# One Trainium2 core, an audio tower block: where the input x and its parts enter

## The chip, the cores and the metric

The kernel runs on one core of a Trainium2 chip. The time is device microseconds of one execution. Five engines work side by side and meet at semaphores: TensorE (PE; its weight loads are PEld), VectorE (DVE), ScalarE (ACT), GpSimd (POOL) and SyncE (SP). SP only issues DMAs; ACT issues some as well. The DMAs of all queues are carried out by 16 DMA engines.

## The reference, cut to what matters

x has the shape (32, 4, 250): 32 sequences, 4 input dims, 250 positions. The first layer makes from it a state of 64 values for each position and refines it 8 times, from the left and from the right:

```python
a = jnp.einsum('bdl,od->blo', x, W1) + b1
for _ in range(8):
    up = relu(a + shift_r(up) @ W2.T + b2)
    down = relu(a + shift_l(down) @ W2.T + b2)
c = jnp.einsum('bdl,od->blo', x, W3) + b3
miu = relu(c + (shift_r(up) @ W4.T + b4) + (shift_l(down) @ W4.T + b4))
```

After it come a residual attention layer with 8 heads whose scores are exp(-gamma * squared distance), and a residual mixture of experts (16 experts, top 2) with a layer norm. Only the first layer reads x.

## The kernel before, in words

The work has three stages: A (the first layer, L964 to L1049), B (attention) and C (experts). The trace has A up to about 106 us. The change is all in the stretch before A's loop has got going.

The products with x are made in bfloat16 without losing float32 precision: x is split into PARTS = 3 bfloat16 parts whose sum is x, and the weights are too. Each x term is one matmul over XROWS = 3 * 3 * 4 = 36 rows (every part of x against every part of the weights, for 4 dims) and 3 further rows that hold a constant for the bias. So rows 0 to 35 and 64 to 99 of the tiles `xa` and `xw` hold x (the second half in reversed order of positions), and rows 36 to 38 and 100 to 102 a constant, ONES2. Rows 32 to 63 and 96 to 127 are filled with the constant first, and the x rows are then written over them by DMA.

How x gets there:

1. SP issues the load of x into `x_in` (L265). Behind it, on the same queue, it issues the seven A_LOADS (L267): `c_sb`, `aw1_sb`, `aw2_sb`, `cw1_sb`, `cw2_sb` (these four are 103 rows of 256 bytes), `w24_sb` and `gam_sb`.
2. DVE fills rows 96 to 127 of `xa` and `xw` (L657, L658), then waits for x and splits it into `x_part` in four steps (L661 to L667). POOL fills rows 32 to 63 (L330, L331), then makes 24 small fills at the edges of the state tiles (L335 to L338; PREP_GA counts them), then two long fills of `m2` (L341).
3. SP waits for the split and for POOL's two fills (PREP_GX), writes `x_part` to the DRAM buffer `xparts` (L271), waits until it has landed, and issues four reads of it for round 0 (`replicate`, L277): `xa` in two halves and `xw` in two halves. Each read writes 36 partitions. Its source has the shape [3 copies, 12 rows, n * 500 elements], where the 12 rows are (part, dim). Behind them SP issues the eleven B_LOADS (L287), and then the four reads of round 1.
4. ACT waits for x, issues the four W_LOADS (L490), waits for PREP_GA and then relieves PSUM. The instruction ACT_TABLE_LOAD stands ahead of its first activation (L498).
5. DVE waits for all A_LOADS and makes the bfloat16 parts of the first layer's weights (L670 to L676, PREP_A = 5). Then, in `weights()` (L680 to L692, PREP_W = 8), it waits for PE's weight products and takes them out of PSUM (L688, L691). Only then does it relieve PSUM in stage A (L700).
6. PE waits for the W_LOADS, makes the weight products (L966, L967), waits for PREP_A and PREP_GA, and begins stage A. `step_a` (L995) with k = 0 waits for the reads into `xa`, and for lane 3 for PREP_W; with k = 1 it waits for both evacuations of its lane (a_sa by ACT, a_sb by DVE) and for the reads into `xw`. There are 4 lanes and 2 rounds.

Of the kernel before, what the change touches and what calls it, by code (L numbers as in the profile page):

```python
# [8 lines left out]
ACT = mybir.ActivationFunctionType  # L9
AX = mybir.AxisListType  # L10
F32 = mybir.dt.float32
# [4 lines left out]
B, D_IN, L = 32, 4, 250  # L16
# [9 lines left out]
C = 2 * L  # L26
# [10 lines left out]
PARTS = 3  # L37
XROWS = PARTS * PARTS * D_IN
AROWS = XROWS + PARTS
HALF = 64  # L40
XK = HALF + AROWS
ONES2 = 1.0019378662109375
# [12 lines left out]
def constants():  # L55

    c = np.zeros((128, C_COLS), np.float32)
    c[:, C_IDENT:C_IDENT + 128] = np.eye(128)

    for half in (0, HALF):  # L60
        for part in range(1, PARTS):
            rows = slice(half + part * PARTS * D_IN, half + (part + 1) * PARTS * D_IN)
            for r in (rows, half + XROWS + part):
                c[r, C_W1] = -1.0
                c[r, C_W2] = -1.0 if part == 2 else 0.0
    c[64:, C_MS1] = -1.0
    c[Q_ROW + H:Q_ROW + 2 * H, C_MS2] = -1.0
    c[K_ROW + H:K_ROW + 2 * H, C_MS2] = -1.0
    for a in (1, 3):
        c[a * E:(a + 1) * E, C_MG] = -1.0  # L70
    for h in range(H):
        c[K_ROW + h, C_IND + h] = 1.0
        c[K_ROW + H + h, C_IND + h] = 1.0
    for e in range(E):
        c[e, C_SEL + e * R:C_SEL + (e + 1) * R] = 1.0
        c[E + e, C_SEL + e * R:C_SEL + (e + 1) * R] = 1.0
    return c


def build(nc, cst, xin, xparts, aw1, aw2, cw1, cw2, w24, wqT, wkT, wvT, woT, wq, wk, gam, lns,  # L80
          gw, gb, w1, b1, w2, b2, fg, fb, out):
    with ExitStack() as ctx:
        def sb(name, shape, dt=F32):
            return ctx.enter_context(nc.sbuf_tensor(name, shape, dt))

        def sem(name):
            return ctx.enter_context(nc.semaphore(name))

        def f32(ap):
            return ap.bitcast(F32)  # L90
# [27 lines left out]
        spare, spare2 = sb("spare", [T, 1]), sb("spare2", [T, 1])  # L118
# [55 lines left out]
        ld_w, ld_a, ld_b = sem("ld_w"), sem("ld_a"), sem("ld_b")  # L174
        s_prep = sem("s_prep")
        s_prepg = sem("s_prepg")
        s_wprod = sem("s_wprod")
        a_xin, a_split, a_scr = sem("a_xin"), sem("a_split"), sem("a_scr")
        a_xa = [sem(f"a_xa{i}") for i in range(ROUNDS)]
        a_xw = [sem(f"a_xw{i}") for i in range(ROUNDS)]  # L180
        a_mm, a_sa, a_sb, a_c, a_miu, a_t, a_h = (
# [16 lines left out]
        def full(t):  # L198
            return t[tuple(slice(None) for _ in t.shape)]

        def wait(eng, s, value):

            if not (isinstance(value, int) and value <= 0):
                eng.wait_ge(s, value)
# [3 lines left out]
        A_LOADS = [(c_sb, cst), (aw1_sb, aw1), (aw2_sb, aw2), (cw1_sb, cw1), (cw2_sb, cw2),  # L208
                   (w24_sb, w24), (gam_sb, gam)]
# [6 lines left out]
        def steps(eng, step, body):  # L216

            first, last = body
            for p in range(first):
                step(p, p % 2, p >= 2, p >= 1, True, True)  # L220
            with eng.Fori(0, (last - first) // 2) as i:
                for k in range(2):
                    step(i * 2 + (first + k), (first + k) % 2, True, True, True, True)
            for p in range(last, PAIRS + 2):
                step(p, p % 2, p - 2 < PAIRS, p - 1 < PAIRS, p < PAIRS, p + 1 < PAIRS)
# [37 lines left out]
        @block.sync  # L263
        def _(sp):
            sp.dma_start(x_in[:, :, :], xin[:, :, :]).then_inc(a_xin, 16)  # L265
            for dst, src in A_LOADS:
                sp.dma_start(full(dst), full(src)).then_inc(ld_a, 16)  # L267

            sp.wait_ge(a_split, SPLIT)
            sp.wait_ge(s_prepg, PREP_GX)  # L270
            sp.dma_start(xparts.rearrange("r p (q l) -> q r p l", q=128), x_part[:, :, :, :]).then_inc(a_scr, 16)  # L271
            sp.wait_ge(a_scr, 16)

            def replicate(dst, half, rev, p0, n, s, d0):
                cols = slice(p0 * C, (p0 + n) * C)
                src = xparts[rev, :, :].rearrange("p (d c) -> (p d) c", d=D_IN)[:, cols]
                sp.dma_start(dst[half:half + XROWS, d0 * C:(d0 + n) * C],  # L277
                             src.unsqueeze(0).to_broadcast([PARTS, PARTS * D_IN, n * C])).then_inc(s, 16)

            for i in range(ROUNDS):  # L280
                for half, rev in ((0, 0), (HALF, 1)):
                    replicate(xa, half, rev, 2 * LANES * i, 2 * LANES, a_xa[i], 2 * LANES * i)
                for half, rev in ((0, 1), (HALF, 0)):
                    replicate(xw, half, rev, 2 * LANES * i + LANES, LANES, a_xw[i], LANES * i)
                if i == 0:
                    for dst, src in B_LOADS:
                        sp.dma_start(full(dst), full(src)).then_inc(ld_b, 16)  # L287


            def duplicate(p, j, u):  # L290
                sp.wait_ge(b_ev, 16 * p + 9 + 2 * u)
                for a in range(2):
                    sp.dma_start(f32(m1[j][64 - 64 * a:128 - 64 * a, 2 * u + a, :]),
                                 f32(m1[j][64 * a:64 * a + 64, 2 * u + a, :])).then_inc(b_dup[u], 16)


            def step_b(p, j, old2, old, new, ln):
                if new:
                    duplicate(p, j, 0)
                    duplicate(p, j, 1)  # L300
                    sp.wait_ge(b_s2, p + 1)
                    wait(sp, b_sc, 16 * (p - 1))
                    for k in range(2):
                        sp.dma_start(f32(m2[j][ONE_ROW + k:ONE_ROW + k + 1, :, :]),
                                     f32(s2[j][Q_ROW + k * H:Q_ROW + (k + 1) * H, :])).then_inc(b_row, 16)
                    duplicate(p, j, 2)
                    duplicate(p, j, 3)

            steps(sp, step_b, BODY_B)


            with sp.Fori(0, PAIRS) as i:
                sp.wait_ge(c_pout, i + 1)
                sp.dma_start(out[ds(i * 2, 2), :, :].rearrange("b (k t) d -> t (b k) d", k=2), res[:, :, :])\
                    .then_inc(c_out, 16)
            sp.wait_ge(c_out, 16 * PAIRS)
# [3 lines left out]
        def _(gp):  # L320
            count = [0]

            def done(ins):

                count[0] += 1
                ins.then_inc(s_prepg, 1)
                gp.wait_ge(s_prepg, count[0])


            done(gp.memset(xa[32:64, :].bitcast(F32), ONES2))  # L330
            done(gp.memset(xw[32:64, :].bitcast(F32), ONES2))  # L331
            assert count[0] == PREP_GX
            for j in range(LANES):
                for t in (st_a[j], st_b[j]):
# [150 lines left out]

        @block.scalar
        def _(act):
            act.wait_ge(a_xin, 16)
            for dst, src in W_LOADS:
                act.dma_start(full(dst), full(src)).then_inc(ld_w, 16)  # L490
# [156 lines left out]
        def _(dve):  # L647
# [6 lines left out]
                dve.wait_ge(s_prep, count[0])  # L654


            dve.memset(xa[96:128, :].bitcast(F32), ONES2)  # L657
            dve.memset(xw[96:128, :].bitcast(F32), ONES2)  # L658

            dve.wait_ge(a_xin, 16)  # L660
            dve.tensor_copy(x_part[:, :, 0, :], x_in[:, :, :]).then_inc(a_split, 1)  # L661
# [589 lines left out]
SPLIT = 4  # L1251
PREP_A = 5
PREP_W = 8
PREP_GX = 2
PREP_GA = PREP_GX + 6 * LANES
PREP_G = PREP_GA + 26
GATE_D = 9
# [72 lines left out]
```

## Time and profile before

| | |
|---|---|
| median of 3 runs | 883.58 us (882.91 to 884.26) |
| profiled execution, time | 883.49 us |
| its span, first to last instruction | 881.3 us |
| PE busy | 799.4 us (91%) |
| DVE busy | 770.7 us (87%) |
| ACT busy | 593.7 us (67%) |
| POOL busy | 458.0 us (52%) |
| mean granted TensorE clock | 0.987 |

The span is cut into 40 slices of 22 us on the page. PE's digit is 1 in the first, 6 in the second and 8 or 9 from the third to the 39th. A slice's digit is the busy share in tenths.

### The profile page before, as it was taken

The page shows a single profiled execution, that of the slowest core. Times are in us where ns is not written, and L with a number is a line of the kernel's source. Part 1 is how long each engine was busy: PE and PEld are TensorE (multiplying, and loading weights), DVE is VectorE, ACT ScalarE, POOL GpSimd, SP SyncE. Part 2 cuts the span into 40 slices and gives each one's busy share as a digit, 9 for nine tenths or more (in the row PEclk, how much of TensorE's full clock was granted, in tenths as well). Part 3 has the DMA queues.
Part 4 walks back from the last instruction along what each step waited for, and adds up shares of the span by engine and source line. Part 5 has one row for each costly group of instructions (what it writes and reads, how often), then busy time and mean ns, then how long its engine had stood idle before and what let it go on. Part 6 is the DMA issues. An engine that isn't in the chain of part 4 may idle for free.

```text
span 881.3 us, 17428 instructions
## 1 busy us (share of the span) xinstructions
PE 799.4 (91%) x4384; PEld 456.0 (52%) x4384; DVE 770.7 (87%) x1970; ACT 593.7 (67%) x1089; POOL 458.0 (52%) x600
## 2 busy tenths in 40 slices
PE   1699879999999999999999998899999999999994
PEld 1244356666666666666666655344444444444441
DVE  5376769999999999999999998899999999999984
ACT  0365678778788788788788775566666666666652
POOL 7270255435445445445544421267776667777655
PEclk9999979999999999999999999999999999999998
DMA  4400022111222111222111220000000000000000
GB/s 115 134 16 2 1 49 47 27 37 38 49 48 48 24 36 36 48 48 48 25 38 34 49 49 1 0 5 9 6 6 6 6 6 7 6 6 6 9 10 12
DMA packets 22742, 25.16 MB, mean 29 GB/s; under 512 B 12753, under 2 KB 21649, under 8 KB 22577
## 3 DMA queue, kind: packets, MB, share of 16 engines
q1 hardware_dynamic: 22384, 23.93, 11.5%
q10 hardware_dynamic: 320, 0.79, 0.4%
q8 instruction: 18, 0.29, 0.1%
q14 instruction: 20, 0.16, 0.1%
HBM read 5.37 MB, written 2.43 MB: 9 GB/s over the span
## 4 chain that ended last, share of the span: by engine, by line
PE 54%; DVE 16%; issue 15%; POOL 7%; ACT 4%; DMA 2%; SPq 1%; POOLq 1%; DVEq 0%; ACTq 0%
PE bank L1178 9%; PE bank L1196 9%; PE bank L1063 8%; PE bank L1111 6%; PE bank L991 6%; PE bank L1087 4%; DVE gated L258 3%; PE bank L1089 3%; DVE prob L773 3%; DVE lg L866 2%; DMA xw<-xparts 2%; DVE m L789 2%; PE bank L981 1%; DVE lg L870 1%; POOL xn L409 1%
## 5 line engine op out<-in xcount | busy, mean ns | idle before, releaser
L773 DVE TENSOR_SCALAR prob<-prob,cap_hi,cap_lo 125x250 f32<-125x250 f32 x512 | 231.4, 500 | 16.9 <-ACT prob L542 14.2
L607 ACT ACTIVATE relu<-bank,b_sb 128x500 f32<-128x500 f32 x256 | 161.1, 675 | 101.5 <-PE bank L1196 86.4
L420 POOL TENSOR_TENSOR sq<-sq 125x256 f32<-125x256 f32 x128 | 97.5, 767 | 166.1 <-ACT sq L556 109.9
L542 ACT ACTIVATE prob<-bank 125x500 f32<-125x500 f32 x256 | 148.3, 590 | 41.0 <-PE bank L1089 37.7
L258 DVE TENSOR_TENSOR gated<-relu,wb 128x500 f32<-128x500 f32 x224 | 159.9, 728 | 7.7 <-ACT relu L607 5.5
L1178 PE MATMUL bank<-gated,w_sb 128*64 128x500 f32 x512 | 136.0, 610 | 12.6 <-DVE gated L258 12.6
L1063 PE MATMUL bank<-prob,u 125*64 125x250 f32 x1024 | 125.0, 382 | 1.9 <-DVE prob L773 1.8
L1087 PE MATMUL bank<-m,s 128*125 128x500 f32 x256 | 110.9, 433 | 4.1 <-issue 1.9
L1196 PE MATMUL bank<-s,w_hi 128*128 128x500 f32 x256 | 110.6, 432 | 0.0
L1089 PE MATMUL bank<-m,s 112*125 112x500 f32 x256 | 101.3, 396 | 0.0
L1196 PE MATMUL bank<-s,w_lo 128*128 128x500 f32 x256 | 99.5, 388 | 0.0
L1063 PEld LDWEIGHTS bank<-prob,u 125*64 125x64 f32 x1024 | 66.2, 136 | 55.3 <-issue 16.8
L789 DVE TENSOR_TENSOR m<-bank,m 64x500 fp32r<-64x500 f32 x128 | 86.3, 674 | 3.7 <-ACT m L551 1.4
L556 ACT ACTIVATE sq<-bank 125x512 f32<-125x512 f32 x128 | 76.2, 600 | 19.5 <-POOL sq L420 16.8
L1111 PE MATMUL bank<-wqku_hi,s 128*125 128x512 f32 x192 | 77.6, 404 | 6.4 <-DVE m L789 3.9
L1196 PEld LDWEIGHTS bank<-s,w_hi 128*128 128x128 f32 x256 | 48.4, 189 | 59.3 <-ACT relu L607 54.4
L1111 PE MATMUL bank<-wqku_lo,s 128*125 128x512 f32 x192 | 76.8, 400 | 0.0
L551 ACT ACTIVATE m<-bank 64x500 fp32r<-64x500 f32 x128 | 74.0, 578 | 0.8
L1087 PEld LDWEIGHTS bank<-m,s 128*125 128x125 f32 x256 | 48.0, 187 | 36.9 <-issue 29.3
L700 DVE TENSOR_SCALAR st_b<-bank 128x500 f32<-128x500 f32 x56 | 37.3, 678 | 29.2 <-PE bank L991 22.1
L991 PE MATMUL bank<-st_a,w_sb 64*64 64x500 f32 x224 | 58.7, 594 | 0.0
L991 PE MATMUL bank<-st_b,w_sb 64*64 64x500 f32 x224 | 57.8, 595 | 0.0
(176 smaller groups left out, 1476.8 us busy)
## 6 DMA issues: line engine op xcount, KB each, us to landing
m<-m SPq DMA_DIRECT2D x128, 125.0 KB, 2.3
out<-res SPq DMA_DIRECT2D x16, 125.0 KB
xa<-xparts SPq DMA_DIRECT2D x4, 281.2 KB
w1raw<-in_w SPq DMA_DIRECT2D x1, 1024.0 KB
xw<-xparts SPq DMA_DIRECT2D x4, 140.6 KB
w_sb<-in_w SPq DMA_DIRECT2D x1, 512.0 KB
m<-s SPq DMA_DIRECT2D x32, 15.6 KB
xparts<-x_part SPq DMA_DIRECT2D x1, 375.0 KB, 4.3
```

The lines of the kernel that those rows point to most:

```text
L258: eng.tensor_tensor(gated[g % 8][:, :], relu_sb[g % 4][:, :], wb[j][:, :], ALU.mult).then_inc(s_done, 1)
L542: act.activation(prob[n % PROBS][:, :, :], bank[5 + n % 3][0:T, 0:C].rearrange("p (h l) -> p h l", h=2), ACT.Exp).then_inc(b_exp, 1)
L607: act.activation(relu_sb[g % 4][:, :], bank[4 + g % 4][:, 0:C], ACT.Relu, bias=b1_sb[:, g:g + 1]).then_inc(c_relu, 1)
L773: last = dve.tensor_scalar(part, part, cap_hi[0:T, h:h + 1], cap_lo[0:T, h:h + 1], ALU.min, ALU.max)
L789: last = dve.tensor_tensor(m2[j][0:64, h, :], bank[2 + k % 3][rows, 0:C], f32(m1[j][rows, h, :]), ALU.subtract)
L991: last = pe.matmul(dst[cols, 0:C].rearrange("p (b l) -> p b l", b=2), w24_sb[rows, 0, :], src[rows, :, 0:L], start=False, stop=True)
L1063: last = pe.matmul(bank[1][64 * c:64 * c + 64, 0:L], u_sb[jj][:, 2 * b + c, h * D:(h + 1) * D], prob[(2 * v + c) % PROBS][:, hh, :], start ...
L1087: pe.matmul(ps, s1[o][:, cols], m1[o][:, 2 * hp:2 * hp + 2, b * L:(b + 1) * L], start=True, stop=False)
L1089: pe.matmul(ps, s2[o][:, cols], m2[o][:, 2 * hp:2 * hp + 2, b * L:(b + 1) * L], start=False, stop=True).then_inc(b_sc, 1)
L1111: last = pe.matmul(dst[0:T, :], s1[j][:, c * T:(c + 1) * T], w[:, q, :], start=first, stop=not first)
L1178: last = pe.matmul(y[64 * k:64 * k + 64, 0:C], w2_sb[:, g, :], gated[g % 8][:, :], start=False, stop=v == 7, skip_group_check=True)
L1196: last = pe.matmul(bank[4 + g % 4][:, 0:C], w[:, g, :], s1[o][:, :], start=first, stop=not first)
```

## The change

A_LOADS are issued by ACT as its first instructions; SP's queue then holds x_in, the write of `xparts` and the reads. ACT does one activation of a single column ahead of its wait for x; DVE clears that column for it. POOL makes all four fills of constant rows (PREP_GX = 4) and DVE none. SP waits for POOL's fills behind the landing of `xparts`, no longer ahead of its write. The source of each read has the shape [12 rows, 3 copies, n * 500]: the three copies of a row now lie in neighbouring partitions, and the rows of the weights (`stacked`) and of the constants are laid out to match.

```diff
-            rows = slice(half + part * PARTS * D_IN, half + (part + 1) * PARTS * D_IN)
+            rows = slice(half + part, half + XROWS, PARTS)
@@ block.sync
             sp.dma_start(x_in[:, :, :], xin[:, :, :]).then_inc(a_xin, 16)
-            for dst, src in A_LOADS:
-                sp.dma_start(full(dst), full(src)).then_inc(ld_a, 16)
-
             sp.wait_ge(a_split, SPLIT)
-            sp.wait_ge(s_prepg, PREP_GX)
             sp.dma_start(xparts.rearrange("r p (q l) -> q r p l", q=128), x_part[:, :, :, :]).then_inc(a_scr, 16)
             sp.wait_ge(a_scr, 16)
+            sp.wait_ge(s_prepg, PREP_GX)
@@ replicate
-                             src.unsqueeze(0).to_broadcast([PARTS, PARTS * D_IN, n * C])).then_inc(s, 16)
+                             src.unsqueeze(1).to_broadcast([PARTS * D_IN, PARTS, n * C])).then_inc(s, 16)
@@ block.gpsimd
-            done(gp.memset(xa[32:64, :].bitcast(F32), ONES2))
-            done(gp.memset(xw[32:64, :].bitcast(F32), ONES2))
+            for rows in (slice(32, 64), slice(96, 128)):
+                done(gp.memset(xa[rows, :].bitcast(F32), ONES2))
+                done(gp.memset(xw[rows, :].bitcast(F32), ONES2))
@@ block.scalar
+            for dst, src in A_LOADS:
+                act.dma_start(full(dst), full(src)).then_inc(ld_a, 16)
+            act.wait_ge(a_table, 1)
+            act.activation(spare2[:, :], spare[:, :], ACT.Relu)
             act.wait_ge(a_xin, 16)
@@ block.vector
-            dve.memset(xa[96:128, :].bitcast(F32), ONES2)
-            dve.memset(xw[96:128, :].bitcast(F32), ONES2)
+            dve.memset(spare[:, :], 0.0).then_inc(a_table, 1)
@@ constants and stacked()
-PREP_GX = 2
+PREP_GX = 4
-                o[r * HALF:r * HALF + XROWS] = np.tile(w.T, (PARTS * PARTS, 1))
+                o[r * HALF:r * HALF + XROWS] = np.tile(np.repeat(w.T, PARTS, axis=0), (PARTS, 1))
```

## Rows read from the trace of the kernel before

**Rows 1.** Chain of waits, start and length in us, and what
```profile
10.74 4.34 DMA xparts<-x_part
...
15.10 0.87 SPq L277
...
17.47 14.42 DMA xw<-xparts
...
32.02 0.59 PE bank L981
...
32.66 1.67 PE bank L991 x8
...
38.72 0.84 PE bank L991 x8
```

**Rows 2.** Timeline of SP's queue: start us, us, engine, line, operation
```profile
0.76 0.41 SPq L265 DMA_DIRECT2D x_in<-in_xin  x1
...
2.82 3.32 SPq L267 DMA_DIRECT2D cw_sb<-in_cw  x2
...
6.19 3.96 SPq L267 DMA_DIRECT2D w_sb<-in_w  x1
...
10.19 0.43 SPq L267 DMA_DIRECT2D gam_sb<-in_gam  x1
```

**Rows 3.** Timeline of ACT and its queue
```profile
3.48 0.56 ACTq L490 DMA_DIRECT2D wqv_sb<-in_wqT  x1
...
5.42 0.62 ACTq L490 DMA_DIRECT2D wko_sb<-in_woT  x1
...
26.92 1.28 ACT L498 ACT_TABLE_LOAD   x1 [26.92 <-PE bank L984]
```

**Rows 4.** Timeline of DVE and POOL, idle time before and its releaser in brackets
```profile
0.75 3.42 POOL L330 MEMSET xa<- 32x4000 f32 x1 [0.29 <-POOLq L1319]
...
5.41 1.73 DVE L658 MEMSET xw<- 32x2000 f32 x1 [0.36 <-issue]
...
6.04 0.11 POOL L335 MEMSET st_a<- 128x2 f32 x1
...
7.15 0.42 DVE L661 CAST x_part<-x_in 128x500 bf16<-128x500 f32 x1
...
8.77 0.68 DVE L667 TENSOR_TENSOR x_part<-x_res,x_part 128x500 bf16<-128x500 f32 x1
...
10.07 0.10 POOL L338 MEMSET sh<- 64x2 f32 x1
...
10.23 6.91 POOL L341 MEMSET m<- 32x4000 f32 x2
...
14.99 2.23 DVE L672 CAST awr<-awt 103x128 bf16<-103x128 f32 x1
...
17.64 0.23 DVE L675 CAST awr<-awt 103x128 bf16<-103x128 f32 x1
...
19.45 0.68 DVE L691 COPY wraw<-bank 128x512 f32<-128x512 f32 x1
...
26.97 2.44 DVE L700 TENSOR_SCALAR st_b<-bank 128x500 f32<-128x500 f32 x4 [6.84 <-PE bank L984]
```

**Rows 5.** Stretches: busy time of each engine, PEclk, DMA share, GB/s
```profile
9.00:9.50 0.50, 0.00 (x0) 0.00 (x0) 0.45 (x1) 0.00 (x0) 0.33 (x4) 1.00 0.07 19
...
22.00:22.50 0.50, 0.00 (x0) 0.00 (x0) 0.00 (x0) 0.00 (x0) 0.00 (x0) 1.00 0.15 64
...
128.00:132.00 4.00, 4.00 (x11) 3.10 (x10) 3.17 (x11) 3.11 (x7) 0.23 (x1) 0.52 0.00 0
```

**Rows 6.** DMA issues on the page: KB each
```profile
xa<-xparts SPq DMA_DIRECT2D x4, 281.2 KB
```

**Rows 7.** Groups by line, 11 to 26 us: busy, mean ns, idle before
```profile
L966 PE MATMUL bank<-wko_sb,wqv_sb 64*128 64x64 f32 x16 | 3.7, 420 | 11.8 <-DMA wko_sb<-in_woT 11.8
```

**Rows 8.** Waits, 34 to 110 us: total us, times, longest
```profile
POOL inv L390 <- DVE aggr L738: 27.9, 1, 27.9
```

More of the change, by code:

```diff
@@ L177, in build @@
         s_wprod = sem("s_wprod")
-        a_xin, a_split, a_scr = sem("a_xin"), sem("a_split"), sem("a_scr")
+        a_xin, a_split, a_scr, a_table = sem("a_xin"), sem("a_split"), sem("a_scr"), sem("a_table")
         a_xa = [sem(f"a_xa{i}") for i in range(ROUNDS)]
```

## The prediction

> **What bounds the kernel now.** I began with the page's busy digits: PE is at 1 and 6 in the first two slices and at 8 or more afterwards, so the part of the kernel that the change touches is a stretch in which PE waits. Then the chain of waits over the first 80 us [rows 1]. It says what PE waited for: SP issues its loads, `xparts` is written (10.74, 4.34 us), the four reads are issued from 15.10, and the last of them, into `xw`, is waited for 14.42 us. From 32.02 on the chain lies on PE without a gap until stage A ends near 106 us. So whatever moves the first matmul of step k = 1 (now 32.02) moves everything behind it by the same amount, until another engine or load is late. That instant is what I compute.
>
> Three more views say what each part of the wait is made of. The timeline of SP's queue [rows 2] shows that issuing alone keeps SP busy from 0.76 to 10.62: one load, `w24`, holds it for 3.96 us. The stretch of 9.00 to 9.50 [rows 5] lies in it: DMA share 0.07, which is about one of 16 engines (0.0625), at 19 GB/s. The queue is held by transfers that one engine does. The timeline of DVE and POOL [rows 4] shows that x was split late, 7.15 to 9.45, because DVE filled rows until 7.14. And the stretch at 22.00 [rows 5], in which only the reads are under way, has share 0.15, at most three engines of 16, and 64 GB/s.
>
> **The reads.** They have 3 outer copies before and three engines' worth of traffic; 12 outer rows should give 12 engines. The four of round 0 move 843.6 KB, or 864,000 bytes (two of 281.2 KB into `xa` [rows 6], two of half that into `xw`). They take from the first issue at 15.10 to 32.02, which is 16.9 us. At 64 GB/s this volume needs 13.5 us, so 3.4 us are issue and latency. With four times the engines the transfer takes 13.5 / 4 = 3.4 us, and the last issue now matters: the four issues take from 15.10 to 17.43. I expect the last read about 5.7 us after the first issue; bounds 3.4 (transfer free) and 16.9 (nothing gained).
>
> The Trainium skill, DMA: Bandwidth & Descriptors, section "Why a DMA increments its semaphore by 16 and not by 1", says that a DMA from SP or ACT runs on the largest number of engines up to 16 that divides the slowest dimension of both sides: 3 of (3, 36) before, 12 of (12, 36) after. By that rule the trace's 0.15 agrees (3/16 is 0.19), and 103 rows, a prime, go on one engine, which agrees with the 0.07. Its section "Issuing engines are not separate DMA queues" speaks against the other edit: issuing from a second engine saves only sequencer time, "usually small relative to the DMA itself". By that rule the queue edit moves nothing: the reads would start at 15.1 as now, the last land 5.7 later at 20.8, and W_LOADS be no later than now, so k = 1 at 20.9, 11.1 us earlier, and 870.9 with the clock's share below. The trace disagrees about "small": SP's issue of the seven loads takes 9.4 us. I give this case no more than 2 in 100.
>
> **x, its split and the fills.** x lands by 3.48, when ACT, which waits for it, issues its first load [rows 3]. DVE no longer fills 5.1 us of rows first. But POOL now fills all four: 3.42 + 1.76 + 3.42 + 1.76 us and gaps, from 0.75 to about 11.3 (DVE's fill of `xw` took 1.73, POOL's 0.03 more) [rows 4]. Do DVE's casts and POOL's fills run side by side? L672's cast took 2.23 us, from 14.99 to 17.22, and POOL's long fill ended at 17.14; the equal cast of L675 took 0.23 [rows 4]. So a cast between two SBUF tiles waits until POOL's fill is over. Worked out: first cast from 3.5 ends at 4.6 (behind the fill that ends at 4.17), subtraction to 5.3, second cast behind the fill of `xw` (now to 6.4) ends at 6.8, last subtraction at 7.5. POOL's fills lose 0.4 us twice and end at 12.0. The write of `xparts` is issued at 7.5 and takes 4.34 as now: landed at 11.9. Then SP waits for the fills, 12.0. The reads start at 12.0 in place of 15.10 (bounds 10.2, if nothing collides and the fills alone decide at 11.3 or less; 13.5, if every cast waits for a long fill). The last one has landed at 12.0 + 5.7 = 17.7.
>
> **What is late next: the weight products.** So far k = 1 could start at 17.8, a gain of 14. It can't, for what I expect of ACT's queue. W_LOADS are issued now from 3.48 to 6.04 [rows 3], the products wait for them until 11.84 and take 3.7 us [rows 7]. After the change they stand behind seven A_LOADS and the activation with its table load.
> - ACT's seven issues: at most SP's 9.4 us (0.8 to 10.2), since their one-engine transfers then ran against W_LOADS on that engine, which now come later; at least seven at 0.6 us, the length of ACT's own [rows 3], to 5.0. `cw1` and `cw2` held SP for 3.32 us and `w24` for 3.96 [rows 2]; I take 8.3, nearer to the upper end.
> - Table load 1.28 us [rows 3] and a short activation, 0.2: W_LOADS start at 9.8.
> - From their first issue to the products: 8.4 us now (3.48 to 11.84), of which a part is the shared engine. At least 2.6 us of issuing and 2.7 as x_in took (0.76 to 3.48), 5.3. They now meet the `xparts` write and the first reads. I take 6.4: products start at 16.2.
> - Products 3.7: 19.9. DVE's L691 takes 0.68 [rows 4] and L688, of the same 128x512 from PSUM, as much: 21.3. DVE's first evacuation, a quarter of 2.44 [rows 4], with its hand-over: 0.7. So k = 1 starts at 22.0, in place of 32.02: **10.0 us gained**.
>
> Beside this: A_LOADS landed by about 10 to 11, so L670 to L676 (2 us without a blocked cast) end before 14, unless a cast meets a fill. POOL's 24 small fills take 4.1 us (6.04 to 10.17) and end at 16.1: PREP_GA comes before the products end. Its long fills of `m2` then run from 16.1 to 23; DVE has by then only PSUM reads, which the trace doesn't show blocked. The reads into `xa` (17) come before 19.9. The table load is 0 on the path before (hidden in the wait for `xw`) and 1.3 to 1.5 in the chain above. B_LOADS start earlier by about 3 us and finish earlier; POOL's preparation has 27.9 us of idle time behind it [rows 8], so nothing of it comes on the path.
>
> **The clock.** The two first steps of k = 1 run at half rate: eight L991 matmuls take 1.67 us against 0.84 later [rows 1], 2.1 us lost with their x terms. That is the 1.2 GHz level, behind a wait of PE for `xw`. After the change PE is busy from 16.2 to 21 with products and x terms, with short gaps, so the clock may already be full at 22.0, or rise a step or two later. Bounds 0 and 2.1, I take 1.5. Further on there are half-rate stretches at the seam of A and B, like 128 to 132 with 0.52 [rows 5]. Where they fall may shift by a few us; a shift of a stretch by 3.4 us is worth 1.7 us, either sign. Mean 0.
>
> **Sum.** 10.0 + 1.5 = 11.5 us off the profiled execution's 883.49 (span 881.3 and 2.2 around it): 872.0. The median of the runs, 883.58, is 0.1 above that execution; I leave it.
>
> **Rivals.**
> 1. ACT's queue is as slow as SP's was: issues to 10.2, table to 11.7, products 8.4 later at 20.1, k = 1 at 25.9. Gain 6.1, no clock gain: 877.4. For it: the one-engine transfers are the same. Against: their competitor on that engine is gone while they run.
> 2. The reads stay as narrow: last one at 12.0 + 16.9 = 28.9, gain 3.1, 880.4. For it: the bytes and destinations are unchanged, and 36 destination rows may be the limit. Against: the share 0.15 for three copies and 0.07 for 103 rows.
> 3. **Slower.** W_LOADS, queued behind A_LOADS, come so late that the products end behind 32. This decides from a product start of 26.2, that is a first W issue at 17.8 with 8.4 us behind it: the seven issues would need 15.5 us in place of 9.4. If sharing the first engine with x_in, the `xparts` write and the reads doubled them (18.8), products would start at 29.5, k = 1 at 35.3: 3.3 us slower, 886.8. For it: SP was held for 3.96 us by a single load. Against: 19 GB/s on one engine is a light load, and x needs little of it.
> 4. A_LOADS decide, not W_LOADS: a cast of DVE's preparation is caught behind one or both 3.4 us fills of `m2`. PREP_W comes at 24.5, gain 6.8: 876.7 before any clock gain. For it: L672. Against: it needs A_LOADS later than 14.
>
> **Chances.** Forecast 0.74, the queue edit worth nothing 0.02, rival 1 0.08, rival 2 0.05, rival 3 0.03, rival 4 0.05, and 0.03 for a gain returned at the seam so that less than 0.2% is left. 0.2% (1.8 us) is what a measurement of this kernel can tell from no change. So faster 0.94, same 0.03, slower 0.03. The fast end: issues to 7.0, table to 8.5, products 5.3 later, k = 1 at 19.6, gain 12.4, clock 2.1, seam 1.5: 867.5. The slow end takes in rivals 1 and 4: 877.5.
>
> **What would show it.** In the trace after: the stretch with the reads at a DMA share near 12/16; the `xparts` issue near 7.5 and first read near 12.0; ACT's first W issue near 9.8; products starting near 16.2; the first L991 near 22.0 and waiting for DVE's evacuation, not for a DMA; L991's first eight at 0.84 or a little over. I am wrong if k = 1 waits for `xw`, or if PE's start moves by 10 us and the end doesn't.

## The result: 873.53 us, 10 us faster

The changed kernel takes 873.53 us (median of 4 runs, 873.05 to 874.62) against 883.58 (four runs, 882.91 to 884.26): ratio 0.9888, 95% interval 0.9871 to 0.9905. The forecast was 872.0 with a range of 867.5 to 877.5. The profiled execution took 874.62 with a span of 872.5; against the 881.3 of before that is 8.8 us less. The ratios of the table further down leave out one run of the kernel before, of 1293.1 us at a granted clock of 0.567. The page's first part and PE's digits:

```profile
span 872.5 us, 17430 instructions
PE 799.6 (92%) x4384; PEld 455.4 (52%) x4384; DVE 768.1 (88%) x1969; ACT 593.4 (68%) x1090; POOL 462.6 (53%) x602
...
PE   1999889999999999999999998899999999999994
```

PE's busy time is the same within 0.2 us; its second digit went from 6 to 9. The chain of waits (start, length, what; lines of the kernel are one further on than before) has where stage A starts:

```profile
22.98 0.59 PE bank L982
...
24.86 0.38 PE bank L982
...
25.28 1.67 PE bank L992 x6
...
28.70 0.84 PE bank L992 x7
```

The first four pieces of L982, from 22.98, are step k = 0 of the four lanes; step k = 1 follows without a gap, its first matmul at 24.62 by the timeline, in place of 32.02 [rows 1]. It no longer waits for `xw`; what it waits for is `xa`, since k = 0 comes only at 22.98. The last group of transpositions of stage A starts at 98.31 in place of 106.21. So 7.9 of the 8.8 us are there when stage A ends; the rest comes later, in pieces of 0.4 us and less. The timeline of the stretch, each with its engine, answers to [rows 2 to 4]:

```profile
0.76 0.42 SPq L265 DMA_DIRECT2D x_in<-in_xin  x1
...
4.23 1.76 POOL L329 MEMSET xw<- 32x2000 f32 x1
4.41 1.85 DVE L662 CAST x_part<-x_in 128x500 bf16<-128x500 f32 x1 [3.53 <-DMA x_in<-in_xin]
6.05 3.59 POOL L328 MEMSET xa<- 32x4000 f32 x1
...
7.01 2.90 DVE L666 CAST x_part<-x_res 128x500 bf16<-128x500 f32 x1
...
8.30 0.45 ACTq L487 DMA_DIRECT2D gam_sb<-in_gam  x1
8.79 1.28 ACT L489 ACT_TABLE_LOAD   x1 [8.79 <-issue]
8.87 0.53 ACTq L492 DMA_DIRECT2D wqv_sb<-in_wqT  x1
...
10.66 0.40 SPq L267 DMA_DIRECT2D xparts<-x_part  x1
...
16.08 0.47 PE L967 MATMUL bank<-wko_sb,wqv_sb 64*128 64x64 f32 x1 [16.08 <-DMA wko_sb<-in_woT]
16.64 1.76 SPq L274 DMA_DIRECT2D xa<-xparts  x2
...
22.98 0.59 PE L982 MATMUL bank<-xa,acw 39*64 39x500 bf16 x1 [3.23 <-POOL qkw L340]
```

The products start at 16.08 and end at 19.8; PE then stands idle 3.2 us, until `xa` is there. The trace names POOL's fill of `qkw` as releaser, which no instruction of PE waits for; it is the semaphore event nearest in time. The reads were issued at 16.64, and k = 0 needs those into `xa`. So in this trace x decides, and not the weight products, as the forecast had it. Both casts are long, 1.85 and 2.90 us against 0.42 [rows 4]: each starts inside one of POOL's fills and ends 0.27 us after the fill's end (5.99 and 6.26, 9.64 and 9.91).

The reads themselves are wide now. Stretches, columns as in [rows 5]:

```profile
7.50:8.00 0.50, 0.00 (x0) 0.00 (x0) 0.50 (x1) 0.00 (x0) 0.50 (x1) 1.00 0.08 18
...
19.00:19.50 0.50, 0.50 (x8) 0.50 (x6) 0.00 (x0) 0.00 (x0) 0.50 (x1) 1.00 0.74 240
```

In the second line, 0.74 of 16 engines is 12, at 240 GB/s where it was 64; the first, with only the 103-row loads under way, is about one engine (1/16 is 0.06) at 18 GB/s.

### The profile page after: what moved, and what is told of

It is laid out like the page before. It is cut to its first block, busy times and chain, and to the rows that moved or that the text cites. A ratio compares the mean times of both kernels' runs of the same rounds, so it can differ in the third digit from the quotient of the medians.

```text
span 872.5 us, 17430 instructions
## 1 busy us (share of the span) xinstructions
PE 799.6 (92%) x4384; PEld 455.4 (52%) x4384; DVE 768.1 (88%) x1969; ACT 593.4 (68%) x1090; POOL 462.6 (53%) x602
## 4 chain that ended last, share of the span: by engine, by line
PE 53%; DVE 17%; issue 16%; POOL 9%; ACT 4%; POOLq 1%; DVEq 0%; ACTq 0%
PE bank L1179 8%; PE bank L1197 8%; PE bank L1064 8%; PE bank L1112 6%; PE bank L992 6%; PE bank L1088 4%; DVE gated L258 4%; PE bank L1090 3%; DVE prob L774 3%; DVE lg L867 2%; PE bank L982 2%; DVE m L790 2%; DVE lg L871 1%; POOL xn L407 1%; PE bank L1187 1%
## 5 line engine op out<-in xcount | busy, mean ns | idle before, releaser
L774 DVE TENSOR_SCALAR prob<-prob,cap_hi,cap_lo 125x250 f32<-125x250 f32 x512 | 231.9, 501 | 16.2 <-ACT prob L544 13.5
L1179 PE MATMUL bank<-gated,w_sb 128*64 128x500 f32 x512 | 136.0, 610 | 12.2 <-DVE gated L258 12.2
L558 ACT ACTIVATE sq<-bank 125x512 f32<-125x512 f32 x128 | 76.3, 600 | 20.0 <-POOL sq L418 16.2
L500 ACT ACTIVATE st_a<-bank 128x500 f32<-128x500 f32 x56 | 32.2, 589 | 36.6 <-PE bank L992 23.2
```

Source lines behind the costliest of these rows:

```text
L774: last = dve.tensor_scalar(part, part, cap_hi[0:T, h:h + 1], cap_lo[0:T, h:h + 1], ALU.min, ALU.max)
L1179: last = pe.matmul(y[64 * k:64 * k + 64, 0:C], w2_sb[:, g, :], gated[g % 8][:, :], start=False, stop=v == 7, skip_group_check=True)
```

## The experiments

Each was timed in rounds with the kernel before; unless said otherwise each is an edit of the changed kernel. "x terms" is the start of PE's first x matmul, "end of A" the start of the last transpositions of the stage, both from the profiled execution. The kernel before had medians of 883.52 to 883.66 in these rounds. The changed kernel's two sets of runs (873.05 to 874.62, and 870.58 to 872.74) don't overlap: the same program differs by 2.2 us between rounds, so that a difference of 2 us between kernels of different rounds shows nothing.

| kernel | median us | ratio, 95% interval | products | x terms | end of A |
|---|---|---|---|---|---|
| before | 883.58 | | 11.84 | 26.19 | 106.21 |
| changed | 873.53 | 0.9888 (0.9871, 0.9905) | 16.08 | 22.98 | 98.31 |
| changed, again | 871.32 | 0.9859 (0.9844, 0.9874) | 15.35 | 19.20 | 95.78 |
| before + wide reads | 876.13 | 0.9921 (0.9904, 0.9939) | 12.31 | 21.66 | 98.39 |
| the same, again | 876.01 | 0.9916 (0.9902, 0.9929) | 12.25 | 23.03 | 100.32 |
| narrow reads | 879.50 | 0.9962 (0.9945, 0.9979) | 16.13 | 27.35 | 105.31 |
| tensor_tensor split | 873.09 | 0.9891 (0.9873, 0.9909) | 15.40 | 19.67 | 95.23 |
| DVE fills | 873.85 | 0.9896 (0.9878, 0.9914) | 15.56 | 21.81 | 97.73 |
| no early table load | 872.56 | 0.9890 (0.9859, 0.9920) | 16.00 | 20.00 | 97.87 |
| W_LOADS first | 876.02 | 0.9912 (0.9894, 0.9930) | 7.07 | 22.53 | 100.45 |
| full-height fills | 872.60 | 0.9872 (0.9850, 0.9893) | 15.63 | 19.96 | 96.01 |
| W first, full fills, split | 871.74 | 0.9867 (0.9845, 0.9888) | 7.49 | 18.74 | 94.86 |
| padded loads | 871.77 | 0.9866 (0.9842, 0.9890) | 10.42 | 18.95 | 94.95 |
| padded, full fills, split | 870.78 | 0.9852 (0.9837, 0.9867) | 10.66 | 18.82 | 93.62 |

**The width alone, twice.** The kernel before with

```diff
-                             src.unsqueeze(0).to_broadcast([PARTS, PARTS * D_IN, n * C])).then_inc(s, 16)
+                             src.unsqueeze(1).to_broadcast([PARTS * D_IN, PARTS, n * C])).then_inc(s, 16)
```

and the layouts that go with it.

> The kernel before with only the 12 outer rows in the reads (and the matching rows of weights and constants); queues and fills as before. Theory X (the x chain sets the start of stage A, and the width of the reads is nearly all of the gain): reads issued at 15.1 as before, xa landed 6.3 later at 21.4, step k=1 at about 23.1 against 24.65 in the changed kernel, so it is 1 to 2 us faster than the changed kernel, about 872. Theory Q (the queue and fill edits carry a real share): slower than the changed kernel, 876 or more.

Stage A ended as in the changed kernel, yet the times were 2.6 us apart. So both were run again, in the same rounds:

> The kernel before with wide reads alone, once more, in the same rounds as the changed kernel. Its stage A ended at 98.4 as the changed kernel's did (98.3), but its four times had a median of 876.1 against 873.5. Seam theory (the difference lies behind stage A, in where the half-rate stretches of the clock fall, which goes with the run): the two medians come within 1 us. Rival (queue and fill edits are worth 2 us and more): the gap of 2 to 3 us stays.

The gap was 4.7 us (876.01 against 871.32). Theory X and the seam theory fall: the queue and fill edits carry a real share. Of the 12.2 us of this comparison the width, taken first, has 7.5. SP's queue shows what else varies in this kernel, the issue of the 103-row loads. From the second trace:

```profile
1.68 1.77 SPq L267 DMA_DIRECT2D aw_sb<-in_aw  x2
3.50 4.48 SPq L267 DMA_DIRECT2D cw_sb<-in_cw  x2
...
12.04 0.43 SPq L267 DMA_DIRECT2D gam_sb<-in_gam  x1
...
16.41 1.71 SPq L277 DMA_DIRECT2D xa<-xparts  x2
```

The last of them, `gam`, goes out 1.9 us later than in [rows 2], the write behind it too (12.59 against 10.74), and the reads 1.3 us later (16.41 against 15.10). x was split at 9.45 in both, so the queue held its write for 3.1 us here and for 1.3 us there. Off that queue, x is free of it.

**The other edits alone.** The changed kernel with the narrow reads:

> The changed kernel with the reads back at 3 outer copies. Theory X: reads issued at 16.6 as in the changed kernel, the last landed 16.9 later at 33.5, so stage A starts later than before (32.0): about 885, 1 to 2 us slower than the kernel before. Theory Q: the queue and fill edits bring something without wide reads too: 880 or less.

Measured 879.50: theory Q, and about 4 us faster than before by the medians (3.4 by the ratio) without any wide read. The reads were issued at 16.28, 1.2 us later than before, and PE waited for both kinds:

```profile
PE bank L982 <- DMA xa<-xparts: 7.5, 1, 7.5
PE bank L982 <- DMA xw<-xparts: 2.4, 1, 2.4
```

The x terms come at 27.35, and k = 1 when `xw` is there, with its first state matmul at 32.03 (before 32.41). I had added before's 16.9 us; to the first matmul of k = 1 near 31.7 they took 15.4. Its ten times lie in two heaps, 877.4 to 878.7 (five) and 880.3 to 882.7 (five). The profiled one (881.7) is of the upper, with x split at 10.6 as in the first changed trace.

**The casts.** Both casts of the split as two-input operations with the same result:

```diff
-            dve.tensor_copy(x_part[:, :, 0, :], x_in[:, :, :]).then_inc(a_split, 1)
+            dve.tensor_tensor(x_part[:, :, 0, :], x_in[:, :, :], x_in[:, :, :], ALU.max).then_inc(a_split, 1)
```

> The changed kernel with the two casts of the split written as tensor_tensor max of a tile with itself (same values, 0.68 us each in place of 0.42). Lock theory (a cast between two SBUF tiles waits for GpSimd's fill, a two-input operation doesn't): split done at about 7.0 in place of 10.6, xparts written and landed near 11.5, reads start at 11.6, xa landed by 17.5; then the weight products, done at 19.8, with PREP_W at 21.2, bind: k=1 at 21.9, 2.7 us earlier than 24.65: about 870.8. Rival (the two operations are only slower beside fills, or the fills slow any DVE operation): split done at 10 or later, no gain.

The lock theory's step came out: the timeline has no long one, with the same fills beside it.

```profile
4.05 0.68 DVE L662 TENSOR_TENSOR x_part<-x_in 128x500 bf16<-128x500 f32 x1 [3.16 <-DMA x_in<-in_xin]
...
5.47 0.68 DVE L666 TENSOR_TENSOR x_part<-x_res 128x500 bf16<-128x500 f32 x1
...
6.90 0.40 SPq L267 DMA_DIRECT2D xparts<-x_part  x1
...
11.38 1.76 SPq L274 DMA_DIRECT2D xa<-xparts  x2
```

The write goes out 3.8 us earlier than in the first changed trace, and stage A ends 3.1 us earlier, at 95.23. Not all of that is the edit's: x was there at 4.05 in place of 4.41, and against a trace of the changed kernel in which it was there at 4.02 (below) the write is 0.3 and the end of A 0.5 us earlier. In that one a cast inside the same fill of `xw` took 1.23 us, the operation here 0.68. Two more things kept the gain small. POOL's last fill ran from 9.54 to 11.30, and the reads, which need it, went out at 11.38. And `xa` was there at 19.67, not at 17.5 as expected. The median, 873.09, is only 0.4 below the changed kernel's (expected 870.8); the step is shown by the trace, a gain in time is not.

**Fills back on DVE.**

```diff
+            dve.memset(xa[96:128, :].bitcast(F32), ONES2)
+            dve.memset(xw[96:128, :].bitcast(F32), ONES2)
```

> The changed kernel with rows 96 to 127 filled by VectorE again (before the split), PREP_GX back at 2. Lock theory: DVE's fills run beside GpSimd's from 0.9 to 6.0, the split runs 6.0 to 8.4 with only small fills beside it, in place of 4.4 to 10.6: reads start some 2 us earlier, k=1 at 22 to 22.7, about 871.5. Rival (moving the fills to GpSimd is worth its 5 us of DVE time, as the change assumes): slower than the changed kernel by 1 us or more.

Time the same as changed (873.85). The split ran unhindered, though only from 7.27, as DVE started its fills later than expected: 9.60 for the write, 21.81 for the x terms. The write is 1.1 us earlier than in the first changed trace and 2.4 later than in the second. Which of the two places is better depends on the next point. In this trace k = 1 did wait for `xw`, for 0.3 us until 24.02, so it has the only landing of the last wide read that can be seen: 9.1 us behind the first issue at 14.93. Against the kernel before with wide reads, timed in the same rounds, it is 2.3 us faster (873.22 to 874.70 against 875.06 to 876.92), and both fill rows on DVE; what differs is the queue of the A_LOADS, the early table load and the later wait for POOL. So these are worth something without the moved fills. That the moved fills are worth anything is not shown, and no run has the queue edit alone.

**The changed kernel again.**

> The changed kernel once more, to see how its start varies. Two-path theory (in the trace without the early table load x landed 0.5 us earlier and both casts waited for less: split done at 7.1, against 10.6; which fill a cast meets is decided by 0.5 us of x's landing): in this trace the first cast starts between 3.9 and 4.4, and if it starts before 4.2 the split ends near 7.2 and stage A near 95 to 96. Rival (the early activation or its DVE fill moves x): same as the first trace, cast at 4.4, split 10.6, stage A ends at 98.3. Time 873.5 either way within 1.

Here is the same program with x landed 0.4 us earlier:

```profile
4.02 0.43 DVE L662 CAST x_part<-x_in 128x500 bf16<-128x500 f32 x1 [3.14 <-DMA x_in<-in_xin]
4.23 1.92 POOL L329 MEMSET xw<- 32x2000 f32 x1
...
5.20 1.23 DVE L666 CAST x_part<-x_res 128x500 bf16<-128x500 f32 x1
...
7.17 0.40 SPq L267 DMA_DIRECT2D xparts<-x_part  x1
...
12.00 1.77 SPq L274 DMA_DIRECT2D xa<-xparts  x2
...
19.20 0.59 PE L982 MATMUL bank<-xa,acw 39*64 39x500 bf16 x1 [0.17 <-DMA xa<-xparts]
```

The first cast gets in before the fill of `xw` (which POOL now finishes late, 1.92), the second waits only for that fill and not for the next of 3.4 us. The split ends at 7.14 and not at 10.63. Here the reads needed both the write, landed just before 12.00, and POOL's last fill, over at 11.62. The two-path theory holds: of the six traces with these casts and POOL's fills beside them, the four whose first cast starts at 3.91 to 4.15 have the split done by 7.3, the two at 4.41 and 4.49 at 10.63. The expected time was 873.5 within 1; 871.32 is 2.2 below. That is the size of the step at the end of stage A (95.78 against 98.31), but which path the runs without a trace took is not known; that the two heaps of the narrow kernel are the same two paths fits too, and is not shown either. Why x lands later than before (3.48) is open. With W_LOADS issued beside its load, in place of A_LOADS, the first step of the split starts at 3.60 and 3.67 (two traces below), with A_LOADS beside it at 3.91 or later.

**Table load.**

```diff
-            act.wait_ge(a_table, 1)
-            act.activation(spare2[:, :], spare[:, :], ACT.Relu)
```

> The changed kernel without ScalarE's early activation and its wait (the table load then stands ahead of the first evacuation again). In the changed trace the table load (8.79 to 10.07) runs beside the issues of W_LOADS (first at 8.87), so removing it should not bring W_LOADS forward: products start at 16.1 as before. Theory T (the early load saves its 1.28 us on the first evacuation): ScalarE's first evacuation starts at 25.0 in place of 23.7, first L992-type matmul of k=1 at 26.0 in place of 25.0, stage A ends 1 us later at about 99.3, some 874.5. Rival (prediction's step: the table load delays W_LOADS by 1.3 to 1.5 us): products start at 14.8.

Its x took the short path, so it compares with the second changed trace. W_LOADS go out at 8.61 without the table load and at 8.87 or 8.82 with it, in which both stand side by side; the products don't start earlier (16.00). The load now takes 1.28 us ahead of the first evacuation:

```profile
20.73 1.28 ACT L498 ACT_TABLE_LOAD   x1 [20.73 <-PE bank L983]
22.02 2.03 ACT L498 ACTIVATE st_a<-bank 128x500 f32<-128x500 f32 x4
```

The first evacuation starts at 22.02 against 19.94, stage A ends at 97.87 against 95.78. Of these 2.1 us 0.8 were there at the x terms already and 1.4 at k = 1 (22.66 against 21.26), so the table load explains about 0.6; the last 0.7 came behind k = 1, where the slow first groups lasted longer (see the clock, below). The times (872.56 against 871.32 in other rounds) don't settle it.

**W_LOADS first.** The split as above, and ScalarE's two loops of DMAs in the other order, with W_LOADS no longer behind the wait for x:

> The split by tensor_tensor as in the run before, and ScalarE issues W_LOADS ahead of A_LOADS. Theory S (W_LOADS, when they run beside the xparts write or the reads, slow these: 5.9 us for the write in the changed kernel against 4.3 before, 8.3 us for the xa reads in the tensor_tensor run against 6.3): with W_LOADS gone by about 6 the write takes 4.3 to 4.4 and the xa reads 6.3: reads issued at about 11.8, first x term near 18.2, first k=1 state matmul near 20.2, stage A ends near 93.6 (98.3 in the changed kernel): about 869.5. Rival (the reads are slow by themselves, whatever runs beside them): xa lands at 19.7 or later, stage A ends at 95 or later.

A miss, and by neither theory. Products at 7.07, but the A_LOADS stand behind, and POOL's `m2` fills catch both casts of the preparation:

```profile
16.74 0.23 DVE L670 TENSOR_TENSOR awt<-aw_sb 103x64 f32<-103x64 f32 x1 [10.32 <-DMA gam_sb<-in_gam]
17.14 1.47 DVE L672 CAST awr<-awt 103x128 bf16<-103x128 f32 x1
...
19.03 3.06 DVE L675 CAST awr<-awt 103x128 bf16<-103x128 f32 x1
```

PREP_A comes at 22.5, and the x terms with it: 876.02, the slowest of the variants with wide reads on their own queue. This is the prediction's rival 4, made to happen. Whether W_LOADS slow the write and the reads stays open: from its issue to the first read the write took 4.4 to 6.0 us in the nine traces with the new queues in which it decided, 5.1 of them beside A_LOADS (W first with full fills), and 3.8 to 4.4 in the three of the old queue. Here, as in the run with the split alone, the reads went out at 11.38 only because POOL's last fill ended at 11.29.

**Fills of full height.**

```diff
-            for rows in (slice(32, 64), slice(96, 128)):
-                done(gp.memset(xa[rows, :].bitcast(F32), ONES2))
-                done(gp.memset(xw[rows, :].bitcast(F32), ONES2))
+            done(gp.memset(xa[:, :].bitcast(F32), ONES2))
+            done(gp.memset(xw[:, :].bitcast(F32), ONES2))
```

> The changed kernel with one fill of all 128 rows per tile in place of two of 32 rows (two fills in place of four; the x rows are written over by the reads). If a fill's time goes by columns alone: GpSimd's two fills end near 6.4 in place of 11.6. Lock theory: the first cast still waits for the xw fill (to about 6.2), the second meets only small fills: split done at 8.0 to 8.3 in place of 10.6, xparts issued at 8.1, reads at about 13, xa landed near 20.5, stage A ends near 96: about 871.5. Rival (the fill time goes by rows too): fills 4 times as long, worse than the changed kernel.

```profile
0.75 3.43 POOL L327 MEMSET xa<- 128x4000 f32 x1 [0.29 <-POOLq L1319]
4.24 2.03 POOL L328 MEMSET xw<- 128x2000 f32 x1
```

128 rows take what 32 rows take, so two of the four fills were for nothing. x took the short path (reads at 11.70), stage A ended at 96.01 and the median was 872.60, where 871.5 was expected; against the second changed trace (95.78) and its 871.32 no gain is shown. All three edits together:

> tensor_tensor split, W_LOADS first and full-height fills together. Fills end near 6; the write of xparts (near 7.2) and its landing (near 11.6) decide the reads, so stage A should start as with W_LOADS first alone: first x term near 18, stage A ends near 93.5, about 869.5. Rival: the long fills of m2 now run from about 10 to 17 and catch VectorE's two casts of the weight preparation (A_LOADS land near 12): PREP_A only near 17.5 to 18, stage A then starts at 18 to 18.5 because of PREP_A and not because of xa.

Stage A ends at 94.86, the x terms come at 18.74, 0.25 us behind PREP_A (18.49, by A_LOADS that landed at 16.8): 871.74, where 869.5 was expected. The fills of `m2` were over at 16.7 and caught no cast; the rival was right in PREP_A deciding, and not in why.

**Padded loads.** The four loads of 103 rows with 128, the tiles with them; the computation still reads 103:

```diff
-        o = np.zeros((XK, D), np.float32)
+        o = np.zeros((128, D), np.float32)
```

> The changed kernel with the four weight loads of 103 rows padded to 128 rows (25 rows of zeros more; the computation uses 103). One-engine theory (103 rows run on one DMA engine and hold the issuing queue): ScalarE's seven issues end near 4.3 in place of 8.75, W_LOADS are issued from 4.3, products start near 10 in place of 16.1, A_LOADS have landed by about 6. The write of xparts and the reads then no longer meet W_LOADS if the split ends at 10.6 (write 4.4 us, reads at 15.1, first x term near 21.4); with the split done at 7.2 they meet their tail. Stage A ends near 96 to 97: about 872. Rival (the seven issues are slow for another reason, the ScalarE queue itself): issues still end near 8.7, nothing moves.

```profile
2.18 0.94 ACTq L487 DMA_DIRECT2D cw_sb<-in_cw  x2
3.15 0.46 ACTq L487 DMA_DIRECT2D w_sb<-in_w  x1
3.63 0.45 ACTq L487 DMA_DIRECT2D gam_sb<-in_gam  x1
...
10.42 0.47 PE L967 MATMUL bank<-wko_sb,wqv_sb 64*128 64x64 f32 x1 [10.42 <-DMA wko_sb<-in_woT]
```

`cw` issues in 0.94 us in place of 4.64, `w24` in 0.46 in place of 1.40, and the products start 5.7 us earlier than in the first changed trace, 4.9 earlier than in the second. The one-engine theory holds. The time, 871.77, is that of the changed kernel in the same rounds (871.32): in its second trace x came 0.2 us behind the products, so with these gone x decides at once, 18.95 against 19.20, and k = 1 moves from 21.26 to 20.60. With the split and the full fills:

> Padding, tensor_tensor split and full-height fills together. x chain: split done at 6.9, write meets W_LOADS (data 5.5 to 9.5) and lands near 12, reads take 6.3 to 7: first x term near 18.5; products done near 14; A_LOADS near 6, so VectorE's casts come before the m2 fills. Nothing but the x chain is left: first k=1 state matmul near 20.3, stage A ends near 93.5 against 98.3: about 869. Rival (what stage A gains is given back at the seam to stage B): stage A ends near 93.5 but the time stays above 871.5.

The best start, with the end of A at 93.62, and the lowest median, 870.78; but 0.5 us under the changed kernel, with 870.6 to 872.7 and 869.6 to 872.0, is no difference shown; the expected 869 was missed, and the rival's 871.5 was not reached either. Only 0.8 of its lead at the end of A was there at k = 1 (20.50 against 21.26). The other 1.4 us is in how soon the state matmuls ran at full rate, here from the second group on:

```profile
21.12 1.61 PE bank L991 x8
...
22.95 0.84 PE bank L991 x8
```

Of the 2.2 us that its trace has over the second changed trace at the end of A, the spans (869.9, 870.6) keep 0.7. The rest goes behind stage A: 0.8 more at the seam to B, 1.1 from C's first matmul on, while B gives 0.4 back. Why there, no run tells.

## Why the prediction was right

**The reads** (forecast: four times as wide, last one 5.7 us after the first issue). Right in kind: 0.74 of the engines. In size they are slower: `xa` alone took 6.3 us in the first trace and up to 7.2 in the second, in which they meet W_LOADS; k = 1 waited for `xw` in neither, but all four took 9.1 us in the one trace that shows it (DVE fills). The term was too small because it added the issues of before, 2.3 us, and a quarter of the transfer, 3.4, and nothing for the time from an issue to the data; in before's 3.4 us of issue and latency it had been contained. The Trainium skill's rule on the slowest dimension (DMA: Bandwidth & Descriptors, "Why a DMA increments its semaphore by 16 and not by 1") gave 12 and 1 engines; the traces have 0.74 and 0.08 of 16, and padding 103 to 128 took the issue from 4.64 to 0.94 us.

**The split and the fills** (forecast: a cast waits for a fill; write at 7.5, reads at 12.0). The second trace has 7.17 and 12.00, the last by the write (4.83 us, forecast 4.34) and not by the fills, which ended at 11.62 and not at 12.0. In the first, x was there for the cast at 4.41, behind the start of the next fill at 4.23, and the same rule gives another schedule: 10.66 for the write. I had put x at 3.48; it came at 4.02 and 4.41. And I had let one order of events stand for the kernel, though a cast gets in only at the gap of 0.06 us between POOL's first two fills (4.17 to 4.23), and has to be there by then. My bound of 13.5 for the reads was passed, by 3.1 us, also because the write took 5.98 in place of 4.34.

**The products** (forecast 16.2, DVE's first evacuation behind PREP_W, k = 1 at 22.0). Measured 16.08 and 15.35. In the second trace k = 1 is at 21.26, and the chain of waits has what the forecast named, DVE's evacuation:

```profile
20.48 0.69 DVE st_b L701
...
21.26 0.59 PE bank L982
...
21.89 1.67 PE bank L992 x6
...
23.97 1.67 PE bank L992 x6
...
27.23 0.84 PE bank L992 x7
```

That 16.2 met 16.08 is luck, since its parts were off and cancelled: the table load, which I had put at 1.5 us ahead of W_LOADS, costs them nothing, since ACT's queue issues beside it; and ACT's seven issues took until 8.75 and W_LOADS 7.2 and 6.5 us from their first issue, not 8.3 and 6.4.

**The clock** (forecast: 1.5 us back). Not borne out. The first state matmuls still take 1.67 us for a group, twice the later 0.84, in both traces. Their x terms follow each other at 0.42 us for 500 columns, which is 1.2 GHz; but the granted clock of the view reads 1.00 in every stretch of the first 40 us, before as after, so the level is inferred from the durations, here and in the prediction. Stage A's end moved by 7.9 where k = 1 moved by 7.4, and by 10.4 where it moved by 10.8: 0.5 and -0.3. PE had been busy with products until 19.8 and then idle for 3.2 us in the first; in the second it had been busy since 15.35, the gap was 0.2 us, and the rate had still not risen at k = 1. The term was not a fixed one: over the fourteen traces the first group at full rate starts 2.5 us (padded, full fills, split) to 6.7 us (no early table load) behind k = 1, and 4.6 before, with no order by the edits that the traces show. From k = 1 to the end of stage A they take 73.1 (padded, full fills, split) to 75.2 us (no early table load), 74.2 before. So the 1.5 us had the right size for the best case, but not for the changed kernel, and about 2 us of any difference at the end of A can be this alone.

**The sum.** 10.0 + 1.5 forecast; 7.4 + 0.5 + 0.9 = 8.8 in the first trace; 10.8 - 0.3 + 0.3 (behind A) = 10.7 in the second, whose span is 870.6. So the time came out in the range by two routes. In the second trace the path was the forecast one, with k = 1 at 21.26 for 22.0 and the clock's share at nothing. In the first, which is of the runs that were forecast, x decided and k = 1 came 2.6 us late (24.62 for 22.0): there the wait that I had named was wrong, and when the products ended did not matter.

**The rivals:** the queue never was as slow as feared (issues end at 8.75, forecast 8.3), the reads did not stay narrow, nothing came near 32. Rival 4 happened only where A_LOADS were made late.

## What to carry to other kernels

Look at the outermost size of every DMA's two sides: 3 copies held the four reads for 15.4 to 16.9 us here, where 12 rows took 9.1, and 103 rows held a queue for 4.6 us, where 128 took 0.9. Before work is moved onto GpSimd, list the casts of VectorE that run beside it; here a saving of 5 us of fills could turn into 3.9 us of waiting, and the choice hung on half a microsecond of a load. When a step is made earlier, look for the second thing its successor waits for: with the casts freed, the reads waited for POOL's last fill. Two traces of one kernel are worth having where such a race is in it.

## What the runs showed of the hardware

- A fill of 128 x 4000 f32 on GpSimd takes 3.43 us, one of 32 x 4000 takes 3.42.
- A two-input operation of VectorE with a bfloat16 result (128 x 500, 0.68 us) isn't held by a GpSimd fill; a cast of the same tile is (0.42 alone, up to 2.90).
- The same with small tiles: casts of 103 x 128, 0.23 us alone, took 3.06 beside the fills of `m2`.
- ScalarE's queue issues DMAs while its table load runs (8.87 within 8.79 to 10.07).
- The reads at 12 engines moved 240 GB/s where 3 moved 64, yet from the first issue to the x terms `xa` took 11.1 us before (15.10 to 26.19) and 6.3 and 7.2 after, not a quarter.
- Two DMAs of 103 rows (`cw`) took 4.64 us to issue on ScalarE's queue, padded to 128 rows 0.94.
- The first groups of state matmuls ran at half rate in all fourteen traces, for one to three groups, the same program's two traces differing in how long.
